# Attention and mixture-of-experts block on one Trainium2 core: attention rebuilt with scores on row halves, values as high|low pairs, normalization moved behind the product, x2 made in place, and the stage unrolled

## The reference, cut to what matters

```
xn  = layernorm(x)                                   # over the last axis
for each batch b and head h (64 rows each):
    qk  = xn[b,h]^T @ ctx[b,h] / sqrt(64)            # 512 queries x 512 keys
    sm  = softmax(qk, axis=keys)
    ret[b,h] = ctx[b,h] @ sm^T                       # 64 x 512
x2  = x + gamma * ret
t   = layernorm(x2), as 2048 rows of 512
out = x2 + sum over the 2 best experts of w_e * down_e(silu(t gate_e) * (t up_e))
         + sigmoid(t . shared_gate) * shared_down(silu(t sw_gate) * (t sw_up))
```

## Time and profile before

| | |
|---|---|
| median of three runs | 927.79 us |
| time of the profiled execution | 931.45 us |
| its span, first to last instruction | 929.1 us |
| mean granted TensorE clock | 0.985 of full speed |
| TensorE matmul busy | 871.1 us (94%) |
| VectorE, ScalarE, GpSimd busy | 571.9, 519.0, 477.9 us |
| attention stage | from 0 to about 284 us |

### The profile page before, as it was taken

How to read it: one execution, slowest core, us unless ns; L and a number is a source line. 1 busy time by engine, 2 the same in 40 slices (tenths; PEclk the granted TensorE clock), 3 DMA queues, 4 the chain that set the end, 5 groups by cost and what they waited for, 6 DMA issues and landing times.

```text
span 929.1 us, 14497 instructions
## 1 busy us (share of the span) xinstructions
PE 871.1 (94%) x4560; PEld 746.0 (80%) x4560; DVE 571.9 (62%) x920; ACT 519.0 (56%) x879; POOL 477.9 (51%) x460
## 2 busy tenths in 40 slices
PE   4798998999998999999999999999999999999993
PEld 3587777877776888888888888888899999999992
DVE  5587878787874653442121212113899999999892
ACT  5588788887884432112111111112688888888881
POOL 5587787878740000004333000000589999999984
PEclk9899999999999999999999999999999999999997
DMA  9435334253553431400032002553954344443542
GB/s 135 86 101 158 116 123 149 97 162 103 161 190 127 134 102 46 136 0 1 1 137 25 0 1 91 187 187 104 335 104 86 74 83 75 79 80 68 91 62 40
DMA packets 70142, 93.77 MB, mean 101 GB/s; under 512 B 16137, under 2 KB 35593, under 8 KB 70098
## 3 DMA queue, kind: packets, MB, share of 16 engines
q1 hardware_dynamic: 60338, 72.73, 26.7%
q0 software_dynamic: 9760, 20.49, 12.4%
HBM read 65.59 MB, written 27.60 MB: 100 GB/s over the span
## 4 chain that ended last, share of the span: by engine, by line
PE 70%; ACT 2%; DVE 1%; issue 1%; DMA 0%; POOL 0%; POOLq 0%; SPq 0%; ACTq 0%; DVEq 0%
PE bank L1347 8%; PE bank L1349 8%; PE bank L1348 8%; PE bank L1414 5%; PE bank L1416 5%; PE bank L1415 5%; PE bank L1361 4%; PE bank L1363 4%; PE bank L1362 4%; PE bank L1439 3%; PE bank L1438 3%; PE bank L1440 3%; PE bank L1371 2%; PE bank L1425 1%; PE bank L1241 1%
## 5 line engine op out<-in xcount | busy, mean ns | idle before, releaser
L1035 DVE TENSOR_TENSOR sg<-bank,sg 128x512 f32<-128x512 f32 x44 | 30.4, 692 | 208.8 <-PE bank L1349 200.0
L1347 PE MATMUL bank<-x_hl,wsp 128*128 128x512 f32 x352 | 137.1, 390 | 0.0
L1349 PE MATMUL bank<-x_hl,wsp 128*128 128x512 f32 x352 | 137.0, 389 | 0.0
L1348 PE MATMUL bank<-x_hl,wsp 128*128 128x512 f32 x352 | 137.0, 389 | 0.0
L593 POOL DMA_INDIRECT slot_rows<-msrc,posi x32 | 36.1, 1128 | 176.2 <-PE bank L1349 169.8
L608 POOL DMA_INDIRECT xg<-x_normed_rows,meta x39 | 39.8, 1021 | 159.7 <-PE bank L1371 142.1
L787 ACT ACTIVATE sg<-bank 128x512 f32<-128x512 f32 x44 | 26.3, 598 | 158.4 <-PE bank L1349 158.4
L687 ACT ACTIVATE pth<-bank 128x512 fp32r<-128x512 f32 x128 | 73.4, 598 | 52.0 <-PE bank L1241 50.4
L933 DVE TENSOR_TENSOR ptl<-bank,pth 128x512 fp32r<-128x512 f32 x128 | 85.9, 682 | 21.1 <-ACT pth L687 20.9
L548 POOL TENSOR_SCALAR pb<-pb,rinv 128x512 f32<-128x512 f32 x128 | 87.7, 699 | 13.2 <-DVE rinv L929 7.8
L794 ACT ACTIVATE hh<-sg 128x512 fp32r<-128x512 f32 x44 | 27.8, 631 | 114.2 <-DVE sg L1035 99.5
(11 more groups left out here) (157 smaller groups left out, 2354.2 us busy)
## 6 DMA issues: line engine op xcount, KB each, us to landing
cd<-in_ctx SPq DMA_DIRECT2D x32, 256.0 KB, 4.8
wex<-in_L_ffn_w_gate SPq DMA_DIRECT2D x8, 704.0 KB, 4.3
wex<-in_L_ffn_w_up SPq DMA_DIRECT2D x8, 704.0 KB, 5.7
xb<-in_x SPq DMA_DIRECT2D x16, 256.0 KB, 4.5
cn<-in_ctx SPq DMA_DIRECT2D x16, 256.0 KB, 3.1
x2b<-in_x SPq DMA_DIRECT2D x16, 256.0 KB, 2.7
x_rows<-x2b SPq DMA_DIRECT2D x16, 256.0 KB, 2.1
x_normed_rows<-x2n SPq DMA_DIRECT2D x16, 256.0 KB, 2.0
```

Source lines behind the costliest of these rows:

```text
L1347: te.matmul(bk[:, :], hi, xhi, start=(h == 0), stop=False)
L1348: te.matmul(bk[:, :], hi, xlo, start=False, stop=False)
L1349: ins = te.matmul(bk[:, :], lo, xhi, start=False, stop=(h == HC - 1))
```

## The change

Stage 1 is rewritten on all engines:

- **Scores on row halves.** The queries' high and low parts (`qh`, `ql`) and the keys' (`kh`, `kl`) are tiles of 128 rows, a head in each half. For one query chunk c there are six matmuls of 64 rows: three products for each of the two heads, written alternately, each head into its own bank. The keys in a second layout (`cd`) are gone.
- **High|low values.** The stationary tile of the values holds the high part of a head in 64 columns and the low part in the other 64. One matmul gives both products, in the two halves of the rows of the bank, so `times_v` is two matmuls. The two halves are added afterwards: ScalarE copies one half (`low_half`), VectorE adds it to the other (`halves`), once a head. The fourth product, low values with low probabilities, comes with it.
- **Sums on the product.** The probabilities are not multiplied any more. The reciprocals of the sums are spread over 64 columns (`spread`, GpSimd), transposed (`inverses`, TensorE), scaled by gamma by ScalarE, and GpSimd multiplies the product by them (`scaled`).
- **x2 in place.** x lies in a ring of 8 tiles; GpSimd adds the product into it (`residual`), and it is not loaded a second time.
- **Other engines.** The normed x, the queries' high part and the normed x2 move from ScalarE to GpSimd. The maximum is taken for both heads at once. Scores use two pairs of banks, transposes three banks.
- **Order.** Each engine has a `step(i)` that mixes tiles i+2 to i-3; all steps are written out. SyncE's loads wait for places in TensorE's list of transposes (`paced`), one by one. `gate_up` of chunks 0 and 1 is placed between the last steps.

```diff
+            for i in range(-4, NT + 3):
+                step(i)
...
+            def load_x(t):
+                after(sp, g_x2n, t - NX + 1)
+                after(sp, st_x2[t % 2], 16 * ((t - NX) // 2 + 1))
+                sp.dma_start(xb[t % NX][:, :], x_t[t, :, :]).then_inc(ld_x[t % NX], 16)
...
+            load_x(0)
+            load_values(0)
+            load_x(1)
+            load_values(1)
+            load_x(2)
+            small_ones()
+            load_x(3)
+            for i in range(NT + 3):
+                step(i)
...
-            def norm_p(k, s, pair):
...
+            def scaled(t):
+                g.wait_ge(d_att, 2 * t + 2)
+                g.wait_ge(a_Rg, t + 1)
+                gp.tensor_tensor(att[t % 2][:, :], att[t % 2][:, :], rgam[:, :], ALU.mult).then_inc(g_att, 1)
+            def residual(t):
+                g.wait_ge(g_att, t + 1)
+                gp.tensor_tensor(xb[t % NX][:, :], xb[t % NX][:, :], att[t % 2][:, :], ALU.add).then_inc(g_x2, 1)
...
+            def step(i):                                   # GpSimd
+                if there(i + 1):
+                    queries(i + 1)
+                    keys_hi(i + 1)
+                    queries_hi(i + 1)
+                if there(i - 3):
+                    rows_normed(i - 3)
+                if there(i + 1):
+                    queries_lo(i + 1)
+                    keys_lo(i + 1)
+                if there(i - 2):
+                    inverse_deviation(1, i - 2)
+                if there(i + 2):
+                    inverse_deviation(0, i + 2)
+                if there(i):
+                    spread(i)
+                if there(i + 2):
+                    shift(0, i + 2)
+                if there(i - 1):
+                    scaled(i - 1)
+                if there(i - 2):
+                    shift(1, i - 2)
+                if there(i - 1):
+                    residual(i - 1)
...
+            def low_half(t, s):                            # ScalarE
+                act.wait_ge(e_pv, 8 * t + 4 * s + 4)
+                after(act, d_att, 2 * t - 1 + s)
+                lo, hi = slice(DH * (1 - s), DH * (2 - s)), slice(DH * s, DH * (s + 1))
+                sc.activation(lob[hi, :], bO[lo, :], ACT.Copy).then_inc(a_lob, 1)
...
+            def maxima(t, c):                              # VectorE
+                dve.wait_ge(e_s, 8 * t + 2 * c + 2)
+                after(dve, a_exp, 8 * t + 2 * c - 6)
+                ve.tensor_reduce(negmax[:, c, :], bSS[c % 2][:, :, :], AX_X, ALU.max, negate=True).then_inc(d_max, 1)
...
+            def halves(t, s):
+                dve.wait_ge(a_lob, 2 * t + s + 1)
+                after(dve, g_x2, t - 1)
+                r = slice(DH * s, DH * (s + 1))
+                ve.tensor_tensor(att[t % 2][r, :], bO[r, :], lob[r, :], ALU.add).then_inc(d_att, 1)
...
+            def scores(t, par, c):                         # TensorE
+                if c == 0:
+                    pe.wait_ge(ql_done, t + 1)
                     pe.wait_ge(kl_done, t + 1)
-                for q in (2 * pair, 2 * pair + 1):
-                    te.matmul(bS[q][:, :], qs[s][:, q * P:(q + 1) * P], kh[par][:, s, :], start=True, stop=False)
-                    te.matmul(bS[q][:, :], qs[s][:, q * P:(q + 1) * P], kl[par][:, s, :], start=False, stop=True).then_inc(e_s, 1)
+                after(pe, a_exp, 8 * t + 2 * c - 2)
+                terms = ((qh, kh), (qh, kl), (ql, kh))
+                for n, (a, b) in enumerate(terms):
+                    for s in range(2):
+                        r = slice(DH * s, DH * (s + 1))
+                        ins = te.matmul(bSS[c % 2][:, s, :], a[par][r, c * P:(c + 1) * P], b[par][r, :], start=(n == 0), stop=(n == 2))
...
+                v = vs[par][:, c, 2 * s:2 * s + 2, :].rearrange("p a d -> p (a d)")
+                pe.wait_ge(a_pth, 8 * t + n + 1)
+                te.matmul(bO[:, :], v, pth[n % 4][:, :], start=(c == 0), stop=False)
+                pe.wait_ge(d_ptl, 8 * t + n + 1)
+                te.matmul(bO[:, :], v, ptl[n % 4][:, :], start=False, stop=(c == LC - 1)).then_inc(e_pv, 1)
...
-            logits(NT - 2, 0)
+            for i in range(-4, NT + 1):
+                step(i, i // 2, i % 2)
             gate_up(0, 0, 0)
-            rows_T(NT - 1, 1)
-            logits(NT - 1, 1)
+            step(NT + 1, (NT + 1) // 2, (NT + 1) % 2)
+            gate_up(0, 1, 0)
+            for i in range(NT + 2, NT + 3):
+                step(i, i // 2, i % 2)
```

More of the change, by code:

```diff
@@ L206, in xattn_moe_kernel @@
         packed = place("packed", [1, NG])
-        bank = [ctx.enter_context(nc.psum_tensor(f"bank{j}", [P, 512], F32)) for j in range(8)]
-        bS, bT, bO, bM = bank[0:4], bank[4:6], bank[6], bank[7]
+        bSS = [ctx.enter_context(nc.psum_tensor(f"scores{j}", [P, 2, 512], F32)) for j in range(2)]
+        bank = [bSS[j // 2][:, j % 2, :] for j in range(4)]
+        bank += [ctx.enter_context(nc.psum_tensor(f"bank{j}", [P, 512], F32)) for j in range(4, 8)]
+        bO, bT = bank[4], bank[5:8]
+        P_BANK = (0, 1, 0, 2, 0, 2, 0, 2)
         bG, bU, bY = bank[0:2], bank[2:4], bank[4:8]
@@ L285, in there, with over_tiles @@
             return not isinstance(t, int) or 0 <= t < NT
[L287 to L297, removed]
+        def over_tiles(step):
+            for i in range(-4, NT + 3):
+                step(i)
         def over_slots(eng, slot, reads_experts=False):
@@ L346, in load_x2 @@
[L346 to L358, removed]
@@ L587, in _ @@
+            over_tiles(step)
             g.wait_ge(d_r, R_POS)
@@ L1249, in times_v @@
                     pe.wait_ge(d_vl, t + 1)
-                    after(pe, d_x2, t)
-                hi, lo = (vs[par][:, a, c, s:s + 2, :].rearrange("p a d -> p (a d)") for a in range(2))
-                first, last = s == 0 and c == 0, s == 1 and c == LC - 1
-                pe.wait_ge(a_pth, 4 * k + c + 1)
-                te.matmul(bO[:, :], hi, pth[c][:, :], start=first, stop=False)
-                te.matmul(bO[:, :], lo, pth[c][:, :], start=False, stop=False)
-                pe.wait_ge(d_ptl, 4 * k + c + 1)
@@ L1257, in times_v @@
-                te.matmul(bO[:, :], hi, ptl[c][:, :], start=False, stop=last).then_inc(e_pv, 1)
+                if c == 0:
+                    after(pe, d_att, 2 * t + s)
+                v = vs[par][:, c, 2 * s:2 * s + 2, :].rearrange("p a d -> p (a d)")
[3 more added lines that the diff above has]
+                te.matmul(bO[:, :], v, ptl[n % 4][:, :], start=False, stop=(c == LC - 1)).then_inc(e_pv, 1)
@@ L1259, in values_T, with inverses @@
+            def inverses(t):
+                pe.wait_ge(g_rspr, t + 1)
+                for c in range(QC):
+                    ins = te.transpose(bT[1][:, c * P:(c + 1) * P], rspr[:, 2 * c:2 * c + 2, :].rearrange("p s d -> p (s d)"), ident[:, :])
+                ins.then_inc(e_R, 1)
             def values_T(t, half, par):
                 pe.wait_ge(ld_cn[par], 16 * (half + 1))
-                if isinstance(t, int) and t == 2:
-                    pe.wait_ge(d_vl, 2)
-                after(pe, a_lg, t - 2)
```

707 lines of the change are left out of this document (326 added, 381 removed).

## The result

| | before | after |
|---|---|---|
| median of 12 runs each, side by side | 927.61 us | 932.67 us |
| profiled execution, its span | 931.45, 929.1 us | 934.92, 933.2 us |
| first down product | 298.86 | 300.48 |
| TensorE matmul busy | 871.1 us | 864.5 us |
| mean granted clock | 0.985 | 0.975 |

A forecast was written before the change was run, and what follows sets the result against it. TensorE was taken to bound the attention tile (14.5 us plus waits). Start at 28, 15 steps of 14.0, 10.5 and 22 put the first down product at 270.5 against 298.86: 28.3 us saved, 900 us, range 888 to 926.

The forecast's parts named there:

- Order and waits: Attention stage's steady tile: the 18 waits for queries go; waits add 0.9 us to VectorE's 13.1, a 14.0 us step.
- loop through GpSimd: Attention tile: half product, scaling, residual, next queries and keys, scores, maximum and back; 12.1 us, 12.7 with hand-overs.
- The paragraph on loads: Attention stage's loads: x of tile 3 lands at about 28, starting step 1; fewer loads give nothing in steady tiles.
- TensorE, 12.9 us: TensorE's work per attention tile: 12.2 us with score pairs side by side, plus half of 1.3 for shape changes.
- the eight changes of shape: TensorE's switches into and out of 64-row scores, per tile: between nothing and 1.3 us together, half taken.
- VectorE, ScalarE, GpSimd: The other engines' work per attention tile: 13.1 us, some 12.5 us and 10.0 us.
- The end: End of attention stage: last product at 248.5, first down product +22 at 270.5; the deeper pipeline costs 5.5 us.
- All behind it shifts unchanged: Everything after the first down product keeps its length, so the 28.3 us gained carries through to the kernel's time.
- 1 and 2: Rivals on TensorE's scores: pairs run in turn, 924 us, chance 0.13; with drains at shape changes too, 940, chance 0.12.
- Rival 2: TensorE's scores: pairs in turn and every shape change drains; 16.7 us a step, 12 us lost, 940; chance 0.12.
- Rival 3: In-order queues: ScalarE's half-product copies delay exponentials or GpSimd's casts cost 1.3; 1 us more a step, 914; chance 0.16.
- the two signs named for being wrong: Attention stage: score pairs 0.46 us apart from the next pair, or granted clock under 1.00 in steady tiles.

The follow-up runs named there:

- experiment 1: Changed kernel with SyncE's load of tile i+2's values put ahead of the stores of x2 and of the normed rows: 901.96 us, ratio 0.9722.
- experiment 2: Changed kernel with the load of the values ahead of the store of normed rows only, still behind the store of x2: 925.22 us, ratio 0.9962.
- experiment 9: experiment 1's kernel with all 128 rows in each score matmul, wrong results, only timed: 920.38 us, ratio 0.9933.
- experiment 8: experiment 1's kernel with both score matmuls of a pair on rows 0 to 63, wrong results, only timed: 948.35 us, ratio 1.0241.
- Experiment 4: Changed kernel with gate and up of chunk 1 moved behind the last step of the stage: 925.93 us, ratio 0.9975.
- experiment 6: experiment 1's kernel with each head's three score matmuls listed together, not alternately: 901.50 us, ratio 0.9718.
- Experiments 1 to 7: Those numbered here, plus two on the changed kernel: edits of experiment 1 and Experiment 4 together, 893.02 us; these with chunk 2's load earlier, 891.01 us.
- experiment 3: Changed kernel with GpSimd's step opening with the normed rows of x2, ahead of queries and keys: 925.26 us, ratio 0.9979.

## Why the prediction was wrong

**The step that failed** is "Order and waits", with its loop through GpSimd at 12.7 us and its step of 14.0. The loop was drawn from GpSimd through the other engines and back. What the trace of after shows, and experiments 1 and 2 confirm, is a second way around that leaves through SyncE: residual, store of x2, load of the next keys and values behind it, key op. It has 11.5 us on GpSimd and between engines, 0.9 on SyncE and 3.1 in flight, 15.5 together. The edit that makes it was read and priced part by part: the residual moved to GpSimd's end of the step, x2 is stored from there, and each load waits by itself in order. The paragraph on loads then said of them that they "lie beside work in the steady tiles", without asking which wait stands in front of them. Taken out, that loop leaves 13.6 us, and TensorE itself as the bound.

**The sum**, by its own terms, to the first down product: forecast 270.5, measured 300.5. Step 1 starts at 26.3, not 28 (-1.7): the load of x for VectorE's second step was waited for as said, and landed sooner. Fifteen steps take 15.7 on average, not 14.0 (+25.0). From there to the last product it is 13.3, not 10.5 (+2.8); the largest op in it, the tokens' low part, measured 3.37 us where 2.3 was taken (last section). From the last product to the first down product it is 25.9, not 22 (+3.9). All of that lies ahead of the store of the last columns, 17.4 us behind the last product where 13.5 was taken; the granted clock is 0.90 there.

**TensorE, 12.9 us.** Side by side was right, and the pitches of the earlier trace rows gave the rest (15.0 against 14.99 us in experiment 9). The mis-sized term is the eight changes of shape: half of 1.3 was taken, 1.37 measured, so the upper end of the range was the value. With that, scores cost TensorE 2.76 + 1.37 = 4.1 us a tile against 3.7 before, so the row halves alone bring TensorE nothing here. As TensorE is the bound once the loop is gone, 13.6 was the step to forecast. The Trainium skill (TensorEngine Tiling (Array Packing), Key Properties) has both halves of this: tiles operate in parallel, which experiment 8 against 1 confirms, and a switch of mode drains TensorE, with which the 0.17 us of experiments 8 and 9 agree.

**VectorE, ScalarE, GpSimd.** Right: 13.3, 12.8 and 9.8 us. A maximum over two banks measured 1.216 us (1.21 from the earlier trace rows); GpSimd's two-tensor op 1.28, near the low end of the earlier trace rows; the 1.26 that the forecast reads in the earlier trace rows is 1.27 there. The Trainium skill (GPSIMD Engine Reference, section 1's table) has contention where VectorE has two SBUF inputs. In the steady tile its ops have at most one, and the 1.28 us agree.

**The end.** The mechanism was right (nothing left for TensorE to do ahead of the first down product), 7.3 us idle instead of "some 5". What lay outside the forecast is the price behind it: "All behind it shifts unchanged" fails by some 2.5 us at a granted clock of 0.69. Experiment 4 has neither, for 7.6 us.

**The rivals.** 1 and 2 rest on pairs that run in turn, and fall with experiment 8, though 2's price for the changes of shape is real (1.37 us a tile). Rival 2's 940 is not far from the time, for the wrong reason. Rival 3 is the nearest in kind, a wait in an in-order queue; but it named ScalarE's copies and slow casts, where the queue was SyncE's, and it put 1 us on a step where 1.7 came. Its 914 and the whole range down from 926 missed. Of the two signs named for being wrong, the granted clock under 1.00 in steady tiles came, in three steps; the other did not, as pairs follow each other at 0.23 us. With the loop gone the kernel takes 901.96, close to the forecast of 899.5 to 900, but partly by errors that cancel: its steps are 0.4 us shorter than forecast, its end is longer.

**What stays open.** Why do three of the steps take 17.5 to 17.9 us? The trace gives half of an answer. In the one from 68.40:

```profile
75.62 0.61 POOL L539 CAST kh<-cn 128x512 fp32r<-128x512 f32 x1 [4.25 <-DMA cn<-in_ctx]
```

In these three GpSimd waits 4.25 to 4.61 us for the load, against 3.0 to 3.3 in the steps around; TensorE's idle time grows to 2.20 to 2.54 us, and the granted clock falls. In two more steps the load is late too (waits of 3.83 and 4.20 us) while the clock stays at 1.00, and these take 16.1 and 16.5 us. So I estimate that a late load costs 0.6 to 1 us, and the fall of the clock about one more. In experiment 1 nine steps in a row, from 62.82 to 185.36, take 13.6 us each, so all this went with the loop. Why just these loads take longer, no run tells.

## What to carry to other kernels

Before the order of a step is called harmless, go around every loop that a tile makes through the queue that issues loads and stores: a load that stands behind a store inherits what that store waits for, and then its own flight comes on top. Put loads whose buffers come free early ahead of stores of what is just being computed. When a stage gets a deeper pipeline, count what TensorE still has to do between its last product and the first work of the next stage.

## What the hardware showed that was not expected

The two 64-row matmuls of a pair run side by side in both orders of the list that were tried (experiment 6: same step, and both first matmuls in the first place of the group). What brings head 1's forward, in TensorE or ahead of it, the trace does not show.

A change between 128-row and 64-row matmuls costs 0.17 us, as a mean over the eight of a tile (experiments 8 and 9).

VectorE and GpSimd slowed each other. In the kernel after, VectorE's subtraction over 128x2048 meets GpSimd's residual and then its normed rows:

```profile
261.28 3.37 DVE L947 TENSOR_TENSOR x_hl<-x_hl 128x2048 fp32r<-128x2048 f32 x1 [0.89 <-ACT x_hl L710]
```

```profile
261.21 1.28 POOL L566 TENSOR_TENSOR xb<-xb,att 128x512 f32<-128x512 f32 x1
262.48 2.81 POOL L550 TENSOR_SCALAR x2n<-xb,rstd,nmr 128x512 f32<-128x512 f32 x1
```

The normed rows take 0.76 us in every steady step and 2.81 here; VectorE's subtraction takes 2.28 us in its other executions, and the residual its usual 1.28. All of their tensors here are in SBUF. Experiments 1 to 7 have the same place with 3.36 to 3.37 and 2.80 to 2.81 us. The three ops have 1.28 + 2.28 + 0.76 = 4.3 us of work and are done 4.1 us after the first began, nearly as if the engines took turns; that they do is argued from these times, no run was made for it. The prediction weighed this only for GpSimd, and only for the steady tile.

The granted clock fell behind short idle times of TensorE. The kernel after, in the step from 68.40 to 85.93:

```profile
74.83 0.66 PE L1225 MATMUL bank<-ident,pb 128*128 128x128 f32 x4
77.69 1.08 PE L1259 MATMUL bank<-ident,x2n 128*128 128x128 f32 x4 [2.20 <-POOL x2n L550]
78.42 0.77 PE L1239 MATMUL bank<-pth,vs 128*128 128x512 f32 x1
79.00 0.63 PE L1241 MATMUL bank<-ptl,vs 128*128 128x512 f32 x1
```

Behind 2.20 us without work a group of four transposes takes 1.08 us where it took 0.66, and a 512-column matmul 0.63 to 0.77 where it takes 0.39 to 0.50: the level of 1.2 GHz, for some us, in a kernel that is busy nine tenths of the time. The idle time alone does not decide it: in experiment 2 idle times of 2.19 and 2.23 us were followed by no fall, in experiment 3 one of 1.91 was. But a wait in the loop can cost more than its own length.
